# Softmax maxima of the layer attention: ScalarE copies every fourth head's rows to SBUF, VectorE evacuates q, k and v, GpSimd splits the maxima

## The reference

```python
qkv = jnp.einsum('bsd,od->bso', x, W_qkv) + b_qkv
scores = jnp.einsum('bhqd,bhkd->bhqk', q, k) * SCALE
wts = jax.nn.softmax(scores, axis=-1)
o = jnp.einsum('bhqk,bhkd->bhqd', wts, v)
return jnp.einsum('bsd,od->bso', o, W_ao) + b_ao
```

## Time and profile before

| | |
|---|---|
| median of 3 runs | 3266.77 us (3263.84 to 3273.66) |
| profiled execution | 3267.46 us, span 3265.8 us |
| TensorE matmul busy | 2812.3 us, 86% of the span |
| VectorE busy | 1863.4 us, 57% |
| ScalarE busy | 1770.7 us, 54% |
| GpSimd busy | 805.1 us, 25% |
| mean granted TensorE clock | 0.933 |

### The profile page before, as it was taken

How to read it: one execution, slowest core, us unless ns; L and a number is a source line. 1 busy time by engine, 2 the same in 40 slices (tenths; PEclk the granted TensorE clock), 3 DMA queues, 4 the chain that set the end, 5 groups by cost and what they waited for, 6 DMA issues and landing times.

```text
span 3265.8 us, 56810 instructions
## 1 busy us (share of the span) xinstructions
PE 2812.3 (86%) x17396; PEld 1737.5 (53%) x17396; DVE 1863.4 (57%) x3116; ACT 1770.7 (54%) x2669; POOL 805.1 (25%) x864
## 2 busy tenths in 40 slices
PE   7877799787899787898788879999966999799999
PEld 4444446444455444464444446666644777466666
DVE  4567735577546577445677345444536887454444
ACT  6457656367655377654477654444422666544443
POOL 0212200122100222101122014444440000244444
PEclk8989999799899699999799989999987999899999
DMA  2134300244200344101344000000002332000000
GB/s 94 43 94 108 79 6 8 67 100 107 52 12 8 89 103 104 26 8 33 93 99 98 6 7 1 0 0 0 0 1 94 98 101 72 4 4 7 3 6 6
DMA packets 95850, 150.50 MB, mean 46 GB/s; under 512 B 13152, under 2 KB 81248, under 8 KB 89312
## 3 DMA queue, kind: packets, MB, share of 16 engines
q1 hardware_dynamic: 95712, 148.77, 17.3%
HBM read 79.00 MB, written 67.11 MB: 45 GB/s over the span
## 4 chain that ended last, share of the span: by engine, by line
PE 43%; issue 23%; DVE 13%; POOL 11%; DMA 4%; SPq 2%; ACT 2%; DVEq 1%; POOLq 1%; ACTq 0%
POOL hhlo L2179 9%; DVE hmx L1849 9%; PE ps L948 7%; PE ps L754 3%; PE ps L973 2%; PE ps L717 2%; PE ps L681 2%; PE ps L687 2%; PE ps L793 2%; PE ps L829 2%; PE ps L1154 1%; DMA hqk<-hqk_scratch 1%; PE ps L815 1%; SPq L556 1%; DMA hqk_scratch<-hqks 1%
## 5 line engine op out<-in xcount | busy, mean ns | idle before, releaser
L1849 DVE TENSOR_REDUCE hmx<-ps 128x2 f32<-128x512 f32 x1024 | 660.1, 687 | 310.9 <-PE ps L948 310.1
L1445 ACT ACTIVATE hpt<-ps 128x1024 f32<-128x1024 f32 x512 | 522.3, 1024 | 289.5 <-PE ps L960 287.7
L2179 POOL TENSOR_TENSOR hhlo<-hh,hhh 128x512 fp32r<-128x512 f32 x320 | 414.8, 1296 | 463.0 <-ACT hhh L1524 462.1
L948 PE MATMUL ps<-hqk 24*128 24x256 f32 x2048 | 309.0, 359 | 235.1 <-DVE hmx L1849 189.1
L948 PEld LDWEIGHTS ps<-hqk 24*128 24x128 f32 x2048 | 191.5, 206 | 461.8 <-DVE hmx L1849 412.1
L1519 ACT ACTIVATE sil<-ps 128x512 f32<-128x512 f32 x320 | 191.0, 597 | 441.4 <-PE ps L1156 437.4
L1943 DVE TENSOR_TENSOR su<-ps,sil 128x512 f32<-128x512 f32 x256 | 177.1, 692 | 326.7 <-PE ps L1156 318.4
L973 PE MATMUL ps<-hpt,hvx 128*32 128x256 f32 x4096 | 299.3, 413 | 1.9 <-ACT hpt L1445 1.6
L960 PE MATMUL ps<-hqk 26*128 26x256 f32 x2048 | 272.2, 348 | 1.7 <-ACT hpt L1445 1.2
L1524 ACT ACTIVATE hhh<-hh 128x512 fp32r<-128x512 f32 x320 | 199.5, 624 | 40.9 <-DVE hh L1946 26.8
L2136 POOL CAST hqks<-hqk 128x512 fp32r<-128x512 f32 x64 | 40.5, 633 | 673.3 <-ACT hqk L1425 641.8
(11 more groups left out here) (247 smaller groups left out, 5593.1 us busy)
## 6 DMA issues: line engine op xcount, KB each, us to landing
hqk_scratch<-hqks SPq DMA_DIRECT2D x256, 192.0 KB, 3.1
hqk<-hqk_scratch SPq DMA_DIRECT2D x256, 192.0 KB
qk_scratch<-qks SPq DMA_DIRECT2D x16, 768.0 KB, 3.3
k<-qk_scratch SPq DMA_DIRECT2D x16, 384.0 KB
qv<-qk_scratch SPq DMA_DIRECT2D x64, 96.0 KB
mw<-mw_in SPq DMA_DIRECT2D x10, 516.5 KB, 3.9
w12raw<-w_in SPq DMA_DIRECT2D x1, 2560.0 KB, 9.5
streams<-x_in SPq DMA_DIRECT2D x8, 256.0 KB, 4.8
```

What stands on the lines that cost most here:

```text
L948: return mm(ps[:, o % 2, qt * SEQ:(qt + 1) * SEQ], hqk[r][32 * g:32 * g + 24, 0, j, qt * P:(qt + 1) * P], hqk[r][32 * g:32 * g + 24, 1, j, ...
L1445: A(hpt[:, j, g:g + 2, :, :], ps[:, 2 + g:4 + g, :], ACT.Exp, scale=QSCALE).then_inc(hd_exp, 1)
L1849: V.tensor_reduce(hmx[:, r, :, 4 * g + j], ps[:, o % 2, :].rearrange("p (t k) -> p t k", t=2), AX.X, ALU.max).then_inc(hd_max, 1)
L2179: G_.tensor_tensor(hhlo[:, k % 4, :], hh[:, k % 2, :], hhh[:, k % 4, :].bitcast(F32), ALU.subtract).then_inc(e_lo, 1)
```

## The change

In pair steps 1, 3, 5 and 7 the second head's rows (bank 1) are no longer reduced from PSUM. ScalarE copies the bank to a new SBUF tile `hrow` (two buffers) ahead of that step's `exps`, which releases the bank, and VectorE reduces the copy. `hd_max` becomes two semaphores, one per bank. `lay_v` and `evac_qk` move from ScalarE to VectorE, `evac_qk` from after p = 2 to after p = 3. The split of the maxima moves from VectorE to GpSimd (without the negation: the constant rows of `hqk` become -1), and GpSimd's order becomes copy_x, split_max, parts, divide. SyncE's program is as before. The core of the diff:

```diff
+        hrow = at("hrow", [P, 2, 2, SEQ], where=w)
-        hd_max = counter("hd_max", 16)
+        hd_max = [counter(f"hd_max{k}", 8) for k in range(2)]
+        hd_red = counter("hd_red", 4)
 # TensorE, rows() and step()
-                            pe.wait_ge(hd_max, nth(hd_max, B + ahead, o - 1))
+                            for k in range(2):
+                                pe.wait_ge(hd_max[k], nth(hd_max[k], B + ahead, o // 2 - 1))
 # ScalarE
+                def copy_row(b, o):
+                    B = l * BATCH + b
+                    act.wait_ge(hd_am, nth(hd_am, B, o))
+                    act.wait_ge(hd_red, nth(hd_red, B, o // 4 - 2))
+                    A(hrow[:, o // 4 % 2].rearrange("p t k -> p (t k)"), ps[:, 1, :], ACT.Copy).then_inc(hd_max[1], 1)
                     for p in range(8):
+                        ahead, o = (1, 8 + 2 * p) if p < 4 else (2, 2 * p - 8)
+                        if p % 2 == 1 and (n1 if p < 4 else n2):
+                            copy_row(b + ahead, o + 1)
                         exps(b, p)
-                        if p == 0 and n1:
-                            lay_v(b + 1, (r + 1) % 4)
-                        if p == 2 and n3:
-                            evac_qk(b + 3)
 # VectorE
-                def minus_max(b, r):
...
+                def copied_maxima(b, o, r):
+                    B = l * BATCH + b
+                    j, g = ORDER[o] // 4, ORDER[o] % 4
+                    dve.wait_ge(hd_max[1], nth(hd_max[1], B, o // 2))
+                    V.tensor_reduce(hmx[:, r, :, 4 * g + j], hrow[:, o // 4 % 2], AX.X, ALU.max).then_inc(hd_red, 1)
+                def evac_qk(b):
+                    B = l * BATCH + b
+                    dve.wait_ge(hd_qk, nth(hd_qk, B))
+                    dve.wait_ge(hd_parts, nth(hd_parts, B - 1))
+                    for a, bias in enumerate(("bq", "bk")):
+                        V.tensor_scalar(hqk32[:, a, :], ps[:, 7, a * SEQ:(a + 1) * SEQ], T(bias), None, ALU.add)\
+                         .then_inc(hd_q, 1)
+                def lay_v(b, r):
...
                             maxima(b + ahead, o, ra)
-                            maxima(b + ahead, o + 1, ra)
-                        if p == 3 and n1:
-                            minus_max(b + 1, (r + 1) % 4)
+                            if p % 2 == 0:
+                                maxima(b + ahead, o + 1, ra)
+                            else:
+                                copied_maxima(b + ahead, o + 1, ra)
+                        if p == 0 and n1:
+                            lay_v(b + 1, (r + 1) % 4)
+                        if p == 3 and n3:
+                            evac_qk(b + 3)
 # GpSimd
-                    G_.memset(hqk[r][:, 1].bitcast(F32), 1.0)
+                    G_.memset(hqk[r][:, 1].bitcast(F32), -1.0)
+                def split_max(b, r):
+                    B = l * BATCH + b
+                    pool.wait_ge(hd_max[0], nth(hd_max[0], B, 7))
+                    pool.wait_ge(hd_max[1], nth(hd_max[1], B, 7))
+                    pool.wait_ge(hd_red, nth(hd_red, B, 3))
+                    pool.wait_ge(hd_tp, nth(hd_tp, B - 1))
+                    pool.sem_inc(waited, 1)
+                    G_.tensor_copy(hhl[:, :, 0, :], hmx[:, r]).then_inc(hd_mhi, 1)
+                    pool.wait_ge(hd_mhi, nth(hd_mhi, B))
+                    G_.tensor_tensor(hhl[:, :, 1, :], hmx[:, r], hhl[:, :, 0, :].bitcast(F32), ALU.subtract)\
+                      .then_inc(hd_mlo, 1)
                 def step(b, r, first=False, n1=True, n2=True, n3=True):
+                    if n2:
+                        copy_x(b + 2)
+                    if n1:
+                        split_max(b + 1, (r + 1) % 4)
                     if n3:
                         parts(b + 3)
                     if not first:
                         divide(b - 1)
-                    if n2:
-                        copy_x(b + 2)
```

More of the change, by code:

```diff
@@ L952, in rows @@
                 def rows(b, o, r):
-                    pe.wait_ge(hd_max, nth(hd_max, l * BATCH + b, o - 2))
+                    pe.wait_ge(hd_max[o % 2], nth(hd_max[o % 2], l * BATCH + b, o // 2 - 1))
                     row(o, r, 0)
@@ L1484, in head_attention @@
                 evac_qk(2)
+                copy_row(0, 3)
+                copy_row(0, 7)
                 act.wait_ge(hd_bp, nth(hd_bp, l))
                 A(hbo[:], ps[:, 7, 0:1], ACT.Identity, bias=T("bo")).then_inc(hd_bo, 1)
+                copy_row(0, 11)
+                copy_row(0, 15)
                 max_rows(0)
+                copy_row(1, 3)
+                copy_row(1, 7)
                 heads(act, step, lambda: raw(15))
@@ L1849, in maxima @@
                     V.tensor_reduce(hmx[:, r, :, 4 * g + j], ps[:, o % 2, :].rearrange("p (t k) -> p t k", t=2), AX.X,
-                                    ALU.max).then_inc(hd_max, 1)
-                def minus_max(b, r):
+                                    ALU.max).then_inc(hd_max[o % 2], 1)
+                def copied_maxima(b, o, r):
                     B = l * BATCH + b
[L1855 to L1860, removed]
+                    j, g = ORDER[o] // 4, ORDER[o] % 4
[10 more added lines that the diff above has]
+                    B = l * BATCH + b
+                    dve.wait_ge(hd_vp, nth(hd_vp, B))
+                    V.tensor_copy(hvx[r][:].rearrange("p t g j c -> p (t g j c)").rearrange("p (x c) -> p x c", c=64)
+                                  [:, :, 0:48].rearrange("p x (y c) -> p x y c", c=8)[:, :, 0:6:5, :],
+                                  ps[:, 7, 0:SEQ].rearrange("p (x y d) -> p x y d", y=2, d=DH)).then_inc(hd_v, 1)
                 def add_out(b):
@@ L1882, in head_attention @@
                 for o in range(HEADS):
-                    maxima(0, o, 0)
-                minus_max(0, 0)
+                    if o % 4 != 3:
+                        maxima(0, o, 0)
+                    else:
+                        copied_maxima(0, o, 0)
                 for o in range(8):
-                    maxima(1, o, 1)
+                    if o % 4 != 3:
+                        maxima(1, o, 1)
+                    else:
+                        copied_maxima(1, o, 1)
                 heads(dve, step, lambda: None)
@@ L2164, in head_attention @@
                 pool.wait_ge(ln_aff, every(ln_aff, l * (2 * NC) + (NC - 1)))
+                split_max(0, 0)
                 heads(pool, step, lambda: divide(15))
```

## The result

The changed kernel takes 3419.42 us (median of 4 runs, 3413.98 to 3422.41). The kernel before takes 3270.22 us beside it (4 runs, 3263.84 to 3280.04). The ratio is 1.046, 95% interval 1.0435 to 1.0486: 4.6% slower. The forecast, 3366 us with a range up to 3404 us, had the direction right and the size wrong. The profiled execution takes 3417.65 us with a span of 3415.9 us, which is 150.1 us over the 3265.8 us of the earlier trace rows.

A forecast was written before the change was run, and what follows sets the result against it. The prediction saw two near-equal loops, VectorE's reduces with TensorE's rows and SyncE's queue, bounding the kernel. To 3267.46 us it added 64 us for longer sequences and 36 us for the clock: 3367, adjusted to 3366 us, range 3318 to 3404 us.

The forecast's parts named there:

- Odd pair steps: Pair steps with ScalarE's copy of bank 1: 1.50 us for 1.88 us, bounds 1.25 and 1.88 us.
- Copied reduces: VectorE's reduces of the SBUF copies: hidden before the next pair's rows; by the table 0.06 us less per sequence.
- evac_qk on VectorE: Evacuation of q and k behind both reduces of p = 3: the deciding step, ending at T3 + 2.78 us.
- split_max on GpSimd: Split of the maxima ahead of parts: 0.25 us per instruction, done by about T3 + 2.8 us, costing nothing.
- From there to T0': End of evac_qk through parts, spill, send_max and landing to TensorE's next sequence start: unchanged 8.88 us.
- Both loops: In the kernel before, VectorE reduces and TensorE rows (15.0 to 15.5 us) beside the SyncE queue loop (15.2 us).
- Period at full clock: One steady sequence of the changed kernel: 16.92 us, 1.40 us over the mean of 15.52 us.
- The term of +62 us: The 44 steady sequences, sequences 2 to 12 of four layers, each 1.40 us longer without the clock's effect.
- The clock, +36 us: Half clock on TensorE after the wait at T0': +1.1 us in three of four steady sequences.
- Half clock up to T3 in every sequence, with a slow split: Case for the steady sequences: +1.5 us and +0.5 us each, +88 us together, 3419 us; chance 0.10.
- The full-clock case: The SyncE loop lengthens the sequences but TensorE's clock stays up: 3331 us, 3312 to 3345; chance 0.27.
- The rival on the faster side: The pair loop decides at 14.4 us a sequence if evac_qk ends by T0 + 5.5 us: 3213 us; chance 0.05.

The follow-up runs named there:

- e5: The changed kernel with five idle matmuls, results unused, at the end of p = 7 of sequences 0 to 12; 3342.33 us, ratio 1.0244.
- e6: The kernel before with only evac_qk moved to VectorE after p = 3; 3420.82 us, ratio 1.0499.
- e2: The changed kernel with evac_qk back on ScalarE after p = 2, split_max still ahead of parts on GpSimd; 3404.93 us, ratio 1.0442.
- e10: e4 with the two projections exchanged, q and k at p = 0 and v at p = 2; 3203.84 us, ratio 0.9805.
- e4: The changed kernel with evac_qk back on ScalarE after p = 2 and GpSimd's parts ahead of split_max; 3287.17 us, ratio 1.0075.
- e9: e4 with two idle matmuls, results unused, at the end of p = 7; 3244.25 us, ratio 0.9947.
- e7: The changed kernel with evac_qk, lay_v and the split put back, so that only ScalarE's copies remain; 3250.22 us, ratio 0.9971.
- e8: e4 with max_rows ahead of exps at p = 5 and send_max issued from ScalarE's own DMA queue; 3494.76 us, ratio 1.0727.

## Why the prediction was wrong in size

- **Odd pair steps**, 1.50 us expected: 1.44 us at full clock for p = 1 and 3, 1.76 us for p = 5. Even ones took 1.94 us for 1.88 us.
- **Copied reduces**, 0.685 us: 0.688 us, hidden as expected. Here the rows decide against the table on SBUF and PSUM sources that the Trainium skill gives (VectorE: DVE Perf Modes, the section on the TRN2 errata): the reduces from PSUM took 0.689 us. The estimate of 0.06 us a sequence was also that of one copied reduce, where a sequence has four.
- **lay_v**: 0.42 us at p = 0, done 0.6 us before VectorE's next reduce; nothing, as expected.
- **evac_qk on VectorE**, end at T3 + 2.78 us: T3 + 2.72 us in e5; T3 + 3.05 us (766.98) where half clock delays the rows. The step that was said to decide decides: e6 has it alone and loses as much. It isn't the only way to lose, since in e2, without it, the split ahead of parts keeps parts nearly as late (T3 + 2.88 us at full clock).
- **split_max on GpSimd**, 0.25 us for each instruction: 0.21 and 0.25 us, done 0.06 us before evac_qk was, and so before parts could start.
- **From there to T0'**, 8.88 us: 8.93 to 9.0 us in most sequences. hmt stood ready 0.7 us or more ahead of send_max (median 1.55 us), so bank 7 and ScalarE were covered.
- **What sets T0' in the kernel before.** The sequence of the earlier trace rows, with send_max at once behind the spill, is of the rarer kind. In 32 of the 44 steady sequences send_max started 0.03 us behind hmt, 0.3 us after the spill's last issue. Both loops were as near to each other as the text said, so the sum stands.
- **Period at full clock**, 16.92 us: 17.12 us (e5). The term of +62 us was +70 us. Sequences 0 and 1, +8 us: +11.6 us. Sequences 13 and 14, -6 us: -8.0 us.
- **The clock, +36 us, is the term that failed: it was +76 us.** Both factors were too small. The share was put at three sequences of four, and every steady one had a stretch of half clock. The price was put at 1.1 us, and that is right only for the short stretch (T0 to T3 6.45 us for e5's 5.35 us). The long one costs 1.92 us there and 0.3 us more at p = 3, 19.27 - 17.1 = 2.2 us in all. The mean of both kinds, 1.6 us, times 44 is 71 us, the 76 us within 6 us.

The price had been read off two stretches that weren't half clock throughout. The step of the earlier trace rows ends in a row of 0.38 us, so the clock had returned inside it: 2.26 us, where a step wholly at half clock takes 2.60 us. The earlier trace rows is a stretch of 3.4 us, in a layer where only the sequence ahead of it has another, also of 3.4 us. A larger price stood in the fourth layer of the same trace, behind a shorter wait; timeline of TensorE before:

```profile
1640.51 0.38 PE L948 MATMUL ps<-hqk 24*128 24x256 f32 x2 [0.74 <-DMA hqk<-hmt]
...
1644.80 0.58 PE L948 MATMUL ps<-hqk 24*128 24x256 f32 x2
...
1647.53 0.58 PE L948 MATMUL ps<-hqk 24*128 24x256 f32 x2
```

T0 to T3 takes 7.02 us here for 5.64 us, with 6.8 us at half clock, and the sequence is 1.5 us longer than its neighbours. At that price and in every sequence the term comes to 66 us. What the trace of before could not show is what follows when a long wait recurs in every sequence: stretches of 10.2 us.

The case "Half clock up to T3 in every sequence, with a slow split" gave 3419 us, the time measured, at a chance of 0.10. Its first half is what happened; its slow split didn't, and the clock's larger price stood in for it, so that its number is right by luck. The full-clock case (3331 us) is the time that e5 nearly reaches by force (3342 us). By the HAM oscillation rule of the Trainium skill (TensorE: Matmul & The Clock Gate), which ties a fall to longer waits for DMAs than these, the clock would have stayed up in the changed kernel. The trace differs, 0.82, and the row of 1.33 us in the earlier trace rows had been the better guide.

The rival on the faster side named its condition, evac_qk ended by T0 + 5.5 us, and its pair loop of 14.4 us, 3213 us. e10 meets it (evac_qk ends 2.9 us after T0) and measures 14.28 us and 3204 us. The changed kernel had the gain in it, behind the late place of q and k. How much of the 2.0% the copies bring is argued and not shown: no run exchanged the projections without them. The pair steps of the kernel before take 1.88 us each at the least, 15.04 us for eight, which speaks for them.

What is not settled: what decides that one idle stretch is followed by a fall and the next by none. In e4, 1.12 us and 1.14 us at the same place did differently. That the idle time at T0' brings the falls of the changed kernel and of e4 is shown by the fillers: with them the clock stays at 1.00 in all but one of 44 steady sequences in e5, and in all but one in e9. The fillers also raise TensorE's work, but the sum of its idle time doesn't tell the kernels apart: at full clock a sequence has 3.2 us of it in the kernel before and 3.05 us in e4, and the clock falls in 3 sequences of the one and in 23 of the other. The longest single wait is what differs, 0.74 us and 1.09 us in the median. Nor is T0' the only place: the seven falls of e7, which has next to no idle time at T0', all come just behind T5, before which TensorE waits 1.4 us for VectorE. In the changed kernel a long stretch delays TensorE, which then idles less at T0', and the next stretch is short; this could feed itself, but no run tested it, and it doesn't explain e4, where nine sequences kept their clock after 1.07 to 1.14 us of idle time.

## What to carry to other kernels

Where two loops of equal length stand side by side, shortening one gains nothing, so ask first what each moved instruction does to the other: here one evacuation moved to VectorE and a pair step later cost 70 us without the clock. With q and k projected and evacuated two steps earlier than before, the kernel with the copies was 2.0% faster. A wait that recurs in every iteration has two prices, its own length and TensorE's clock after it. Take the second from a stretch that is at half clock from end to end, and count it in every iteration, not in the share of them that shows it while the wait is rare.

## What the runs showed of the hardware

- TensorE's clock fell to 0.50 (1.2 GHz) behind single idle times of 1.1 us (e4) to 2.3 us (the changed kernel) that recurred every 15 to 19 us, and stayed there 3.4, 6.8 or 10.2 us in most cases. In e4 none of the 12 sequences with 0.71 us or less at T0' had a fall, and 23 of the 32 with more had one. With mostly 0.2 us (e5, e9) it fell in one steady sequence of 44, with 0.11 us (e10) in none. But a short wait is no safeguard: in the kernel before it fell three times in the steady sequences, once behind 1.33 us, and once each behind 0.50 and 0.74 us.
- Idle work can make a kernel faster: some 1.03 us of unused matmuls a sequence took 43 us off e4 (3287.17 to 3244.25 us).
- Two DMA issues on ScalarE's queue took 1.13 us, and its next activation started 1.33 us after the one before them (e8). On SyncE, four issues of the spill take 2.58 us, and what stands behind them waits that long.
- GpSimd did a 128x32 cast in 0.21 us and a 128x32 subtraction in 0.25 us, the cast a third of the 0.62 us for 16 times the elements.
- The same subtraction took VectorE 0.19 us with nothing beside it (all 64 in e6). Beside a 128x256 subtraction of GpSimd the order decided. Where GpSimd's had begun 0.01 to 0.06 us earlier, VectorE's took 0.71 to 0.77 us and ended 0.04 to 0.05 us behind it (32 of 64 in the kernel before, 52 of 64 in e7). Where VectorE's began first or within 0.006 us of it (20 in the kernel before), it took 0.19 us, and GpSimd's 0.77 to 0.78 us for 0.73 us.
